# Mamba, MoE and attention on one core: softplus in halves, delta products between half down products, another order of ScalarE's copies and TensorE's turns, and a different start and end of the first stage

## The chip, the cores and the metric

One core of one Trainium2 chip runs the kernel. The metric is the device time in microseconds of one execution; lower is better. The kernel before was timed three times: median 3909.57, from 3905.14 to 3912.57. The engines are TensorE (PE, its weight loads PEld), VectorE (DVE), ScalarE (ACT), GpSimd (POOL) and SyncE (SP), whose instruction stream here issues all DMAs.

## The reference

Two layers are computed for 4096 tokens (batch 2, length 2048) of width 256. All is fp32.

- Mamba block: `xz = norm(x) @ W_in`, split in `x_br` and `z` of width 512; `xb = silu(conv4(x_br))`; `B, C = xb @ W_b, xb @ W_c` (16 states); `delta = softplus(xb @ W_delta + b_delta)`; for each of 16 states `h_t = exp(delta * A) * h_(t-1) + delta * B * xb`, `y = sum(h * C) + xb * D`; `out = (y * silu(z)) @ W_out + x`.
- Mixture of experts: a router (256 to 512, gelu, 512 to 4, softmax), the best two of four experts weigh `gelu(x @ We1) @ We2` (256 to 1024 to 256) per token; residual and norm around it.
- Attention with 16 heads of 16 per batch, keys with an added term from cross products of rotated values and keys, then an FFN (256 to 1024, relu, to 256), each with a norm.

## The kernel before, in words

The program has two blocks, one after the other. `mamba_moe_qkv` does all up to q, k and v; `attention_ffn` the rest. In each, every engine has its own stream, written out by hand and tied to the others by semaphores; each engine runs its stream in order. So a wait at one place holds up all that stands behind it on that engine.

**The chunk loop.** Tokens come in 8 chunks of 512 (`CH`). Features of width 512 are 4 blocks (`DB`) of 128 partitions. `iteration(i)` runs for i = -1 to 9 (3 to 5 in a hardware loop) and treats four chunks at once: i in the scan, f = i + 1 (its projection, conv, B/C and delta), m = i - 1 (out projection, norm 1, router, experts), q = i - 2 (norm 2, v, q, k, cross). It has 16 slots n, one for each state. In a slot DVE does for each of four blocks `b_times` (L1169: du times the broadcast B row, in PSUM) and `scan` (L1176), then `keep_state` (L1182); POOL multiplies by C (L1373) and adds to y (L1384); ACT has computed the decays (L876) one slot ahead; PE broadcasts row n + 2 at the slot's end (L577), for which it waits until DVE has done slot n's products. All other work is hung on slots, by `if n == ...` in each engine's `iteration`:

- **Slot 0:** DVE reads expert 3's down products 6 and 7 of chunk q (`down`, L1254) and computes `gated(m)` (L1188), all behind its scans; PE does these two down products.
- **Slots 1 and 2:** PE `project_out(m)` (L639), which waits for down product 7 to be read; `turn_x2`, `project_v` (L736, L727), `project_z` (L609). ACT `norm2`, `copy_v` (both copies of x2 and of v, L990, L993), `gates` (L890), `norm1` (L113).
- **Slot 3:** PE `project_qk` (turns of v, then q and k), `turn_x1` (L648), `turn_xn` (L586). ACT decays of slot 4 first, then `copy_qk` (v_tok L998, q and k L1005), `copy_x1` (L964), `copy_xn` (L896).
- **Slots 4 to 6:** `project_x(f)` (L597) in two pairs of blocks through PSUM banks 4 and 5, `copy_x` on ACT (L906, L907), `conv` on DVE (L1129, twelve instructions per chunk); cross products and router (L657, L664), logits, weighing. PE adds keys (L781), DVE takes them in slot 7 (`keys`, L1271).
- **Slots 6 to 15:** experts. `up(m, e, half)` (L694): 4 products in 3 side banks, each read by a gelu on ACT (L968); `down(m, e, pair)` (L717): two halves of 16 matmuls. Down products 0, 2, 4, 6 wait for the expert's last two gelus. DVE reads down product j one slot later. Down product 0 also waits for DVE's L1271.
- **Slots 11 to 15:** `project_bc` (L616), and `project_delta` 0 to 3 (L626) in slots 12 and 13, all through bank 5, around one down product in each slot. `copy_delta` on ACT (L928, L929) frees the bank; `softplus` in slot 14 does Exp on both halves (L935), then Ln on both (L939). ACT loads a table when it goes from one of Silu, Gelu, Exp and Ln to another. PE's slot 14 has the fourth expert's first up products and the bias products `base` (L684), which DVE adds in slot 15 (L1241). DVE splits B/C in slot 14 (L1137 to L1144) and computes delta and du at slot 15's end (`deltas`, L1154, L1160).

**The start.** SP loads eight Mamba tensors with x behind the fourth, under one semaphore `w_mamba`; PE, ACT and DVE wait for all of them. DVE's statistics of chunk 0 stand behind that wait. Iteration -1 holds only chunk 0's projection, conv and delta.

**The end.** Iterations 8 and 9 have no scans. In them the attention's first head is begun: `START` says how many steps `start_head` stand in a slot, each two score matmuls on PE (L561) and a maximum over them on DVE (L1110), 49 in all, through one pair of banks; step 36 is a turn (L553), behind which `load_neg` may run. `set_stacks` and `first_loads` (three heads, 13 DMAs each) prepare the operands in iteration 8, slots 3 and 5. The second block begins when the first has ended on all engines, stores included.

The lines that hold the order around the edit:

```python
if n in (12, 13) and inside(f):
    project_delta(f, 2 * (n - 12))
if n in (12, 13) and inside(m):
    down(m, 2, n - 12)
if n in (12, 13) and inside(f):
    project_delta(f, 2 * (n - 12) + 1)
```

## Time and profile before

| what | us |
|---|---|
| median of 3 runs | 3909.57 |
| the profiled execution | 3902.91 |
| its span | 3900.8 |
| busy: PE, DVE, ACT, POOL | 3424.4, 2953.6, 2202.5, 1521.5 |
| weight loads (beside PE) | 1588.6 |
| mean granted TensorE clock | 0.942 |
| first block | 0 to about 2083 |
| one iteration in the hardware loop | 228.66 |

Rows of a timeline read: start, duration, engine, line, operation, output<-inputs, shapes, count; in brackets the engine's idle time before it and who ended it. Neighbouring instructions of one kind are one row, so its duration spans all of them. Matmul ends are modelled and overlap their neighbours. "ps" is PSUM, "stacks", "vals" and "heads_v" are large buffers that hold delta, xb, y and others in the first block, and "hid", "soft", "q_f" are reused as well.

### The profile page before, as it was taken

To read this page: it belongs to the slowest core of one execution; us is meant where nothing else is said; L and a number is where in the kernel's file an instruction comes from. 1 tells how busy PE (TensorE), PEld (TensorE's weight loads), DVE (VectorE), ACT (ScalarE), POOL (GpSimd) and SP (SyncE) were. 2 spreads that over 40 slices of the span, in tenths; PEclk is the share of its full clock that TensorE was granted. 3 is DMA by queue.
4 is the path that set the end of the run, shared out by engine and by line. 5 is a ranking of instruction groups with operands and counts; after the bars stand their busy time and mean duration, and the time that the engine had idled before them with its cause. 6 is when DMAs were issued, how large, how long until landed. Compare 5 with 4: busy or idle time off the path is not lost. (4 is left out here: it accounts for less than half of the span.)

```text
span 3900.8 us, 50068 instructions
## 1 busy us (share of the span) xinstructions
PE 3424.4 (88%) x14561; PEld 1588.6 (41%) x14561; DVE 2953.6 (76%) x3565; ACT 2202.5 (56%) x3624; POOL 1521.5 (39%) x1294
## 2 busy tenths in 40 slices
PE   3238989898898979889988999999999999999898
PEld 1114545455454545546542333323323333333566
DVE  3898787887878788796337888888878888887343
ACT  3436455554646555463215777777777777776221
POOL 0988778787878887797100000000000000000110
PEclk8669999899999989999998999999999999999999
DMA  2111213122121311223301000000000000001010
GB/s 97 33 33 54 60 57 106 57 76 73 55 82 57 106 57 58 69 75 105 107 19 66 18 18 18 18 19 20 22 16 21 18 18 18 18 18 34 22 32 27
DMA packets 110809, 183.02 MB, mean 47 GB/s; under 512 B 14608, under 2 KB 84648, under 8 KB 101866
## 3 DMA queue, kind: packets, MB, share of 16 engines
q1 hardware_dynamic: 110569, 180.13, 14.7%
q8 instruction: 114, 1.87, 0.2%
q14 instruction: 126, 1.02, 0.1%
HBM read 153.99 MB, written 26.09 MB: 46 GB/s over the span
## 5 line engine op out<-in xcount | busy, mean ns | idle before, releaser
L1830 DVE TENSOR_REDUCE tile_max<-ps 128x1 f32<-128x1024 f32 x1028 | 1211.4, 1220 | 246.4 <-PE ps L1621 243.6
L1771 ACT ACTIVATE probs<-ps 128x512 f32<-128x512 f32 x2056 | 1116.1, 598 | 372.4 <-PE ps L1635 346.7
L1373 POOL TENSOR_TENSOR vals<-vals,c_sb 128x512 f32<-128x512 f32 x512 | 685.0, 1369 | 321.7 <-DVE state L1182 321.6
L1176 DVE TENSOR_TENSOR_SCAN vals<-stacks,state,ps 128x512 f32<-128x512 f32 x512 | 655.1, 1280 | 105.9 <-POOL heads_v L1384 36.1
L1635 PE MATMUL ps<-stacks 101*128 101x512 bf16 x2056 | 708.8, 383 | 3.0 <-ACTq L1778 1.7
L1384 POOL TENSOR_TENSOR heads_v<-heads_v,vals 128x512 f32<-128x512 f32 x512 | 638.4, 1278 | 8.7 <-issue 0.2
L1621 PE MATMUL ps<-stacks 99*128 99x512 bf16 x2056 | 615.3, 380 | 0.0
L1645 PE MATMUL ps<-probs,heads_v 128*32 128x512 f32 x4096 | 546.3, 605 | 3.5 <-issue 3.5
L231 POOL COPY heads_v<-vals 128x256 f32 (+1 forms) x32 | 12.6, 400 | 1364.0 <-PE ps L1645 1329.0
L694 PE MATMUL ps<-x1T,e_w 128*128 128x512 f32 x1024 | 489.8, 626 | 58.6 <-ACT hid L968 58.6
L717 PE MATMUL ps<-e_w,hid 128*128 128x256 f32 x2048 | 458.5, 383 | 37.3 <-issue 18.2
L1635 PEld LDWEIGHTS ps<-stacks 101*128 101x128 bf16 x2056 | 198.2, 96 | 639.3 <-ACT probs L1771 431.7
L717 PEld LDWEIGHTS ps<-e_w,hid 128*128 128x128 f32 x2048 | 389.9, 191 | 115.9 <-issue 61.7
L968 ACT ACTIVATE hid<-ps,cols 128x512 f32<-128x512 f32 x288 | 190.2, 686 | 398.7 <-PE ps L694 382.8
L876 ACT ACTIVATE stacks<-stacks,neg_a 128x512 f32<-128x512 f32 x512 | 334.4, 713 | 119.5 <-DVE vals L1176 118.1
L1169 DVE TENSOR_TENSOR ps<-stacks,ps 128x512 f32<-128x512 f32 x512 | 353.9, 691 | 16.2 <-PE ps L577 1.3
L694 PEld LDWEIGHTS ps<-x1T,e_w 128*128 128x128 f32 x1024 | 200.3, 200 | 305.3 <-issue 216.6
L1621 PEld LDWEIGHTS ps<-stacks 99*128 99x128 bf16 x2056 | 201.6, 98 | 180.0 <-issue 2.8
L577 PE MATMUL ps<-bc,sel 96*128 96x512 bf16 x128 | 50.7, 405 | 146.8 <-DVE ps L1169 128.4
L1645 PEld LDWEIGHTS ps<-probs,heads_v 128*32 128x32 f32 x4096 | 80.6, 108 | 197.5 <-ACT probs L1771 178.6
L1254 DVE SCALAR_TENSOR_TENSOR x_tok<-ps,cw,x_tok 128x256 f32<-128x256 f32 x128 | 55.4, 474 | 128.3 <-PE ps L717 128.2
L727 PE MATMUL ps<-x1T,wqkv 128*128 128x512 f32 x192 | 109.0, 723 | 38.0 <-ACT hid L998 25.1
(181 smaller groups left out, 2961.3 us busy)
## 6 DMA issues: line engine op xcount, KB each, us to landing
e_w<-in_e_w SPq DMA_DIRECT2D x64, 1024.0 KB, 7.1
c_sb<-scratch_c SPq DMA_DIRECT2D x128, 256.0 KB, 3.5
stacks<-scratch_q SPq DMA_DIRECT2D x210, 64.0 KB
stacks<-scratch_k SPq DMA_DIRECT2D x210, 64.0 KB
scratch_q<-parts SPq DMA_DIRECT2D x16, 384.0 KB, 4.2
scratch_k<-parts SPq DMA_DIRECT2D x16, 384.0 KB, 4.2
xr<-scratch_x SPq DMA_DIRECT2D x10, 512.0 KB, 4.2
xn_tok<-in_x SPq DMA_DIRECT2D x8, 512.0 KB, 4.8
```

What stands on the lines that cost most here:

```text
L694: last = mm(bank(key), e_w1[:, e % 2, k, i * P:(i + 1) * P], x1T[:, k, :], start=k == 0, stop=k == KD - 1)
L717: last = mm(ps[:, DOWN_BANK[at], i * D:(i + 1) * D], hid[:, k, (2 * pair + i) * P:(2 * pair + i + 1) * P], e_w2[:, e % 2, k, :], start=k = ...
L876: fn(decay[:, n % 2, m, :], delta[:, m, :], ACT.Exp, scale=neg_a[:, n * DB + m:n * DB + m + 1]).then_inc(s["decay_ready"], 1)
L1169: v.tensor_tensor(ps[:, 0, :], du[:, m, :], ps[:, 2 + n % 2, :], ALU.mult).then_inc(s["bx_ready"], 1)
L1176: v.tensor_tensor_scan(h[:, n % 2, m, :], decay[:, n % 2, m, :], ps[:, 0, :], state[:, n, m:m + 1], ALU.mult, ALU.add).then_inc(s["h_ready ...
L1373: last = nc.gpsimd.tensor_tensor(h[:, n % 2, m, :], h[:, n % 2, m, :], c_sb[:, n % C_RING, :], ALU.mult)
L1384: last = nc.gpsimd.tensor_tensor(y[:, m, :], y[:, m, :], h[:, n % 2, m, :], ALU.add)
L1621: last = mm(ps[:, slot(side) + i, :], qs[0:K_MAX, j, t * P:(t + 1) * P], ks[0:K_MAX, j, k * CH:(k + 1) * CH], start=True, stop=True)
L1635: mm(ps[:, S_BANK[i], :], ks[0:K_ALL, j, step * P:(step + 1) * P], qs[0:K_ALL, j, qc * CH:(qc + 1) * CH], start=True, stop=True).then_inc( ...
L1645: last = mm(ps[qc * VW:(qc + 1) * VW, AV_BANK, :], vh[:, j, step, :], probs[:, step % 2, qc, :], start=step == 0, stop=step == KT - 1)
L1771: fn(probs[:, step % 2, qc, :], ps[:, S_BANK[i], :], ACT.Exp)\
L1830: v.tensor_reduce(tile_max[:, t, half:half + 1], ps[:, slot(side):slot(side) + PAIR, :].rearrange("p a n -> p (a n)"), AX.X, ALU.max).then ...
```

## The change

- `deltas` between half products: in slots 12 and 13 PE does a delta product, half a down product, a delta product, the other half.
- Softplus in halves: Exp and Ln of blocks 0 and 1 stand behind `copy_delta(2)` in slot 13, those of blocks 2 and 3 in slot 14.
- Gelu waits: a down product's first half waits for the last three gelus one by one at the k-steps that read them.
- Slot 0: DVE does down 6 and `gated` between its second and third block. `project_out` starts when down 6 is read, and waits for down 7 before its second half.
- Slots 2 and 3: ACT copies x2 before slot 3's decays, v_tok before norm 1, then q, xn, half of slot 4's decays, k, x1, the other half. PE turns v, projects q, turns xn, projects k, turns x1, does the first cross product. `turn_xn` no longer waits for chunk m's x1 copy; `project_x` does.
- B/C product: waits for each block's Silu.
- Chunk 0: x is loaded first; small tensors, the x half of W_in and the rest have a semaphore each; the norm does not wait for weights. The x projection has four banks (`FIRST_X`), so have the deltas (`FIRST_DELTA`), without waits between; `norm0(1)` moves to slot 1 of iteration 0.
- The end: steps of `START` move from iteration 9 to 8, and the last five stand in slot 1 of iteration 9; `set_stacks` does head 0 in slot 0, `first_loads` loads it in slot 2, the others follow in slot 5; `load_neg` in slot 3 of iteration 9.

```diff
-START = {(NCH, 8): 6, (NCH, 9): 6, (NCH, 10): 6, (NCH, 11): 4, (NCH, 12): 2, (NCH, 13): 2, (NCH, 14): 4,
-         (NCH, 15): 4, (NCH + 1, 2): 3, (NCH + 1, 3): 4, (NCH + 1, 4): 2, (NCH + 1, 9): M_FIRST - 43}
+START = {(NCH, 6): 4, (NCH, 7): 6, (NCH, 8): 6, (NCH, 9): 6, (NCH, 10): 6, (NCH, 11): 4, (NCH, 12): 2, (NCH, 13): 2,
+         (NCH, 14): 4, (NCH, 15): 4, (NCH + 1, 1): M_FIRST - 44}
+FIRST_X = [4, 5, 6, 7]
+FIRST_DELTA = [0, 1, 6, 7]
+        def x_bank(c, e):
+            return FIRST_X[e] if first(c) else 4 + e % 2
+        def delta_bank(c, m):
+            return FIRST_DELTA[m] if first(c) else 5
...
             def first_loads():
-                sp.wait_ge(sh.sems["setup"], 2)
...
-                for u in range(3):
-                    load_stack(sp, sh, scr, u, u)
+                sp.wait_ge(sh.sems["setup"], 2)
+                load_stack(sp, sh, scr, 0, 0)
+            def more_loads():
+                sp.wait_ge(sh.sems["setup"], 2 * ROT)
+                for u in range(1, 3):
+                    load_stack(sp, sh, scr, u, u)
...
             load_x(0)
-            for t, name in mamba_loads[4:]:
-                sp.dma_start(t[:], a[name]).then_inc(s["w_mamba"], 16)
+            for t, name in small_loads:
+                sp.dma_start(t[:], a[name]).then_inc(s["w_small"], 16)
+            sp.dma_start(w_in[:, :, 0:DI], a["w_in"][:, :, 0:DI]).then_inc(s["w_x"], 16)
+            for t, src in mamba_loads:
+                sp.dma_start(t, src).then_inc(s["w_mamba"], 16)
...
             def turn_xn(c):
-                at_least(pe, s["x1T_ready"], c - 1)
             def project_x(c, blocks):
+                if first(c):
+                    pe.wait_ge(s["w_x"], 16)
+                at_least(pe, s["x1T_ready"], c - 1)
...
             def project_bc(c):
-                pe.wait_ge(s["xb_ready"], (c + 1) * DB)
                 for k in range(DB):
+                    pe.wait_ge(s["xb_ready"], c * DB + k + 1)
...
             def project_out(c):
-                at_least(pe, s["down_read"], c * 2 * NE)
+                at_least(pe, s["down_read"], c * 2 * NE - 1)
                 for i in (2, 3, 0, 1):
+                    if i == 0:
+                        at_least(pe, s["down_read"], c * 2 * NE)
...
-            def down(c, e, pair):
+            def down(c, e, pair, parts=(0, 1)):
-                wait_read(pe, c, ("up", e, HB - 2))
-                wait_read(pe, c, ("up", e, HB - 1))
-                for i in range(2):
+                for i in parts:
                     for k in range(HB):
+                        if pair == 0 and i == 0 and k >= HB - len(SIDE):
+                            wait_read(pe, c, ("up", e, k))
...
                     if n == 3:
                         if inside(q):
-                            project_qk(q)
+                            turn_v(q)
+                            project_q(q)
+                        if inside(f):
+                            turn_xn(f)
+                        if inside(q):
+                            project_k(q)
                         if inside(m):
                             turn_x1(m)
-                        if inside(f):
-                            turn_xn(f)
+                        if inside(q):
+                            cross(q, 0)
...
-                    if n in (12, 13) and inside(f):
-                        project_delta(f, 2 * (n - 12))
-                    if n in (12, 13) and inside(m):
-                        down(m, 2, n - 12)
-                    if n in (12, 13) and inside(f):
-                        project_delta(f, 2 * (n - 12) + 1)
+                    if n in (12, 13):
+                        for part in range(2):
+                            if inside(f):
+                                project_delta(f, 2 * (n - 12) + part)
+                            if inside(m):
+                                down(m, 2, n - 12, (part,))
...
-            def softplus(c):
-                act.wait_ge(s["abs_ready"], (c + 1) * DB)
...
+            def soft_exp(c, i):
+                half = slice(2 * i, 2 * i + 2)
+                act.wait_ge(s["abs_ready"], c * DB + 2 * i + 2)
+                fn(soft[:, half], soft[:, half], ACT.Exp, scale=-1.0).then_inc(s["soft_ready"], 1)
+            def soft_log(c, i):
+                half = slice(2 * i, 2 * i + 2)
+                act.wait_ge(s["soft_ready"], c * 4 + 2 * i + 1)
+                fn(soft[:, half], soft[:, half], ACT.Ln, bias=1.0).then_inc(s["soft_ready"], 1)
...
                 for n in range(NS):
+                    if n == 2 and inside(q):
+                        copy_x2(q)
-                        if n + 1 < NS:
+                        if n + 1 < NS and n != 3:
                             decays(i, n + 1)
...
                             gates(i)
+                        if inside(q):
+                            copy_v_tok(q)
                         if inside(m):
                             norm1(m)
                     if n == 3:
                         if inside(q):
-                            copy_qk(q)
+                            copy_qk(q, "q", 0)
+                            copy_qk(q, "q", 1)
+                        if inside(f):
+                            copy_xn(f)
+                        if inside(i):
+                            decays(i, 4, (0, 1))
+                        if inside(q):
+                            copy_qk(q, "k", 0)
+                            copy_qk(q, "k", 1)
                         if inside(m):
                             copy_x1(m)
-                        if inside(f):
-                            copy_xn(f)
+                        if inside(i):
+                            decays(i, 4, (2, 3))
...
+                    if n == 13 and inside(f):
+                        copy_delta(f, 2)
+                        soft_exp(f, 0)
+                        soft_log(f, 0)
+                        copy_delta(f, 3)
+                    if n == 1 and first(i):
+                        norm0(1)
                     if n == 14 and inside(f):
-                        softplus(f)
+                        soft_exp(f, 1)
+                        soft_log(f, 1)
...
+                    if n == 0 and inside(q):
+                        down(q, NE - 1, 0)
+                    if n == 0 and inside(m):
+                        gated(m)
...
-                    if n == 0 and inside(q):
-                        down(q, NE - 1, 0)
-                    if n == 0 and inside(m):
-                        gated(m)
...
-            dve.wait_ge(s["w_mamba"], W_MAMBA)
+            norm0_stats(0)
+            dve.wait_ge(s["w_small"], W_SMALL)
```

## Rows read from the trace of the kernel before

**Rows 1.** Stretches, busy us (instructions) of each engine, then granted clock, DMA share, GB/s.

```profile
core 0: us, PE busy (x) PEld busy (x) DVE busy (x) ACT busy (x) POOL busy (x), PEclk, DMA share, GB/s
1153.25:1267.57 114.32, 96.36 (x301) 53.33 (x299) 101.81 (x129) 67.81 (x103) 93.77 (x82) 0.93 0.16 51
1267.57:1381.91 114.34, 104.03 (x334) 62.94 (x335) 85.84 (x106) 59.15 (x82) 91.08 (x73) 0.96 0.29 93
```

**Rows 2.** Timeline of PE around down product 0 of iteration 5.

```profile
1257.80 7.03 PE L694 MATMUL ps<-x1T,e_w 128*128 128x512 f32 x16
1267.67 0.67 PE L717 MATMUL ps<-e_w,hid 128*128 128x256 f32 x2 [2.84 <-issue]
```

**Rows 3.** Timeline of DVE: keys in slot 7, down product 5, base products.

```profile
1266.31 1.26 DVE L1271 TENSOR_TENSOR k_f<-ps,k_f 128x512 f32<-128x512 f32 x2
...
1359.30 0.88 DVE L1254 SCALAR_TENSOR_TENSOR x_tok<-ps,cw,x_tok 128x256 f32<-128x256 f32 x2 [4.70 <-PE ps L717]
...
1379.58 0.69 DVE L1241 TENSOR_TENSOR x_tok<-ps,x_tok 128x512 f32<-128x512 f32 x1 [4.40 <-PE ps L684]
1381.22 0.69 DVE L1241 TENSOR_TENSOR x_tok<-ps,x_tok 128x512 f32<-128x512 f32 x1 [0.94 <-PE ps L684]
```

**Rows 4.** Timeline of PE: down 2, then slots 13 to 15.

```profile
1299.22 1.10 PE L717 MATMUL ps<-e_w,hid 128*128 128x256 f32 x4 [0.82 <-issue]
...
1348.65 3.70 PE L626 MATMUL ps<-vals,w_delta 128*128 128x512 f32 x8 [1.14 <-ACT soft L929]
...
1359.09 3.60 PE L626 MATMUL ps<-vals,w_delta 128*128 128x512 f32 x8
...
1373.69 3.78 PE L694 MATMUL ps<-x1T,e_w 128*128 128x512 f32 x4 [5.63 <-ACT hid L968]
...
1381.11 9.20 PE L694 MATMUL ps<-x1T,e_w 128*128 128x512 f32 x16
```

**Rows 5.** Timeline of ACT in slot 14 of iteration 5.

```profile
1363.31 0.68 ACT L929 ACTIVATE soft<-ps,cols 128x512 f32<-128x512 f32 x1
1363.88 2.55 ACT L876 ACTIVATE stacks<-stacks,neg_a 128x512 f32<-128x512 f32 x4
1366.33 1.99 ACT L935 ACTIVATE soft<-soft 128x1024 f32<-128x1024 f32 x2
1368.34 1.28 ACT L939 ACT_TABLE_LOAD   x1
1369.64 2.00 ACT L939 ACTIVATE soft<-soft 128x1024 f32<-128x1024 f32 x2
```

**Rows 6.** Line L1129, what DVE waited for, us and times: iteration 2, then 5.

```profile
  ACT vals L907: 9.1, 4
...
  ACT vals L907: 3.6, 4
```

**Rows 7.** Timeline of PE in slot 3 of iteration 5.

```profile
1209.90 7.75 PE L727 MATMUL ps<-x1T,wqkv 128*128 128x512 f32 x12 [4.18 <-ACT hid L998]
```

**Rows 8.** Timeline of all engines in the first 60 us.

```profile
13.73 1.40 DVE L100 BATCH_NORM_STATS2 ln_stats<-xn_tok 128x6 f32<-128x256 f32 x4
...
33.02 5.40 PE L597 MATMUL ps<-xnT,w_in 128*128 128x512 f32 x8 [4.34 <-DVE vals L1129]
...
43.02 2.19 ACT L913 ACTIVATE vals<-vals 128x512 f32<-128x512 f32 x4 [2.42 <-POOL vals L1423]
...
57.36 3.70 PE L626 MATMUL ps<-vals,w_delta 128*128 128x512 f32 x8 [1.36 <-ACT soft L929]
```

**Rows 9.** The page's DMA issues: KB each, median us from issue to landing.

```profile
xn_tok<-in_x SPq DMA_DIRECT2D x8, 512.0 KB, 4.8
```

**Rows 10.** Timelines of PE (three rows) and SP in iterations 8 and 9.

```profile
1905.22 0.60 PE L561 MATMUL ps<-stacks 99*128 99x512 bf16 x2
...
2020.23 1.97 PE L736 MATMUL ps<-ident,x_tok 128*128 128x128 f32 x8 [6.72 <-ACT x_tok L113]
...
2080.26 1.03 PE L561 MATMUL ps<-stacks 99*128 99x512 bf16 x2 [1.32 <-DVE tile_max L1110]
...
2070.19 0.95 SPq L461 DMA_DIRECT2D scratch_k<-parts  x2
```

More of the change, by code:

```diff
@@ L620, in project_delta @@
             def project_delta(c, m):
-                if m == 0:
+                if m == 0 and not first(c):
                     pe.wait_ge(s["bc_copied"], c + 1)
-                else:
+                elif not first(c):
                     pe.wait_ge(s["abs_ready"], c * DB + m)
                 for k in range(DB):
-                    last = mm(ps[:, 5, :], w_delta[:, k, m * P:(m + 1) * P], xb[:, k, :],
+                    last = mm(ps[:, delta_bank(c, m), :], w_delta[:, k, m * P:(m + 1) * P], xb[:, k, :],
                               start=k == 0, stop=k == DB - 1)
@@ L869, in _, with decays @@
             fn = nc.scalar.activation
-            def decays(c, n):
-                for m in range(DB):
+            def decays(c, n, blocks=range(DB)):
+                for m in blocks:
                     if n == 0 and m == 0:
@@ L999, in copy_qk @@
                             bank(("v_tok", i)), ACT.Copy), ("v_tok", i))
-                act.wait_ge(s["bc_steps"], 5 * (c + 3 if not isinstance(c, int) else min(c + 3, chunks)))
-                for j, (name, dst) in enumerate((("q", q_f), ("k", k_f))):
+            def copy_qk(c, name, m):
+                j, dst = (0, q_f) if name == "q" else (1, k_f)
+                if name == "q" and m == 0:
+                    act.wait_ge(s["bc_steps"], 5 * (c + 3 if not isinstance(c, int) else min(c + 3, chunks)))
+                if m == 0:
                     at_least(act, s["parts_steps"], 8 * c - 4 + 4 * j)
-                    for m in range(KD):
-                        wait_full(act, c, (name, m))
-                        read(fn(dst[:, m, :], bank((name, m)), ACT.Identity,
-                                bias=col("b" + name, m)), (name, m))
+                wait_full(act, c, (name, m))
+                read(fn(dst[:, m, :], bank((name, m)), ACT.Identity, bias=col("b" + name, m)), (name, m))
             def copy_cross(c):
```

115 lines of the change are left out of this document (60 added, 55 removed).

## The prediction

> **What bounds the kernel now.** The profiled execution took 3902.9 us, with a span of 3900.8. I read the page first, then DVE's idle times with their releasers, then TensorE's and ScalarE's timelines at those places, for the chunk loop, the start and the end of the first stage. The attention stage behind 2083 us has no edited line that runs in it.
>
> In the loop one iteration takes 228.66 us, and it falls into two legs that [rows 1] show with their busy times. I call "base" the moment at which DVE has added the second half of the bias product (1153.25, 1381.91), and "keys" the end of DVE's L1271 (1267.57). Leg A, base to keys, 114.3 us: DVE is busy for 101.8, PE for 96.4. PE's first down product of a chunk starts 0.10 us after L1271 ends, after 2.84 us of idleness: up to there DVE leads [rows 2, 3]. Leg B, keys to base, 114.3 us: PE is busy for 104.0, DVE only for 85.8, and DVE waits for PE, 4.70 us before it can read down product 5, then 4.40 and 0.94 before the base products [rows 3]. So time is won in leg A only by removing DVE's waits, in leg B only on PE's way to what DVE reads next.
>
> **Leg B.** (1) PE's order now is delta 0, down 4, delta 1; delta 2, down 5, delta 3. The new order puts delta 3 ahead of down 5's second half: DVE gets down 5 later by one delta product, 3.60 us [rows 4]. Against that, PE's wait of 1.14 before delta 2 goes, as half a down product (as many columns as a delta product) covers ScalarE's two copies, and the wait of 0.82 before down 2 goes, as its first five k-steps no longer wait for the last gelu [rows 4]. DVE reads down 5 now 91.7 us after keys (1359.30 - 1267.57), then 91.7 + 3.6 - 1.14 - 0.82 = 93.4.
> (2) From that read to DVE's arrival at base lie 15.9 us of its own work (1375.18 = 1379.58 - 4.40, less 1359.30), then two adds of 0.69 [rows 3]. That gives base at 93.4 + 15.9 + 1.5 = 110.8 if PE's base product is ready by 109.3.
> (3) Is it? Now the fourth up product waits 5.63 us for gelu, since ScalarE does both Exps (1.99 for two), an Ln load (1.28), two Lns and a Gelu load behind delta 3 [rows 4, 5]. In halves, Exp and Ln of blocks 0 and 1 take some 3.3 us and run while PE does delta 3. Behind it stand: copies 1.3, Exp load 1.28, decays 2.55, Exp 1.0, Ln load 1.28, Ln 1.0, Gelu load 1.28, one gelu 0.7 = 10.4. Delta 3 is over 95.1 us after keys now, then 95.1 - 3.6 (half a down product less ahead of it) - 2.0 (the two waits) = 89.5. So the fourth up product starts at about 100, with 1 of wait in place of 5.63, and PE does not fall to the lower clock there. Two products of some 1.9 later, at 104, base is ready, 5 us early. So the removed wait is mostly not paid out: DVE, delayed at down 5, is late next. Leg B gains 114.3 - 110.8 = 3.5 us. Bounds: -1.5 (all of (1)'s delay and none of its savings) and 5.3, what DVE now waits at base.
>
> ScalarE has two more table loads per chunk. The row has the load at 1.28 and the next activation right behind it (1368.34 + 1.28 = 1369.62, start 1369.64) [rows 5]. The Trainium skill (ScalarE: Activation LUTs, What ACT_TABLE_LOAD costs) gives about 2.66 us for a switch, a drain of 1.38 included; [rows 5] show no drain. By the skill's figure the start of the kernel, where this chain is bare, would be 2.8 us longer, and the loop the same.
>
> **Leg A.** (4) DVE waits four times per chunk for ScalarE's copies of the x projection: 9.1 us in iteration 2, 3.6 in iteration 5 [rows 6]; the same view gives 5.3, 3.5 and 5.7 for iterations 3, 4 and 6, together 27.2, and none in iterations 0 and 1. The new order (xn turned behind q, copied ahead of k and half of the decays, v's copies ahead of norm 1, which removes PE's wait of 4.18 [rows 7]) brings the x projection forward by 6 us. By my count its copies end 3 us before DVE gets there. I take 20 of the 27, as part may turn into waits for POOL. Bounds 10 and 27.
> (5) The price: PE does not need less time in leg A, so it waits longer for keys, 2.84 + 3 = some 5.8 us. The clock's rows: after 2.84 idle, no fall; after 4.18, twelve matmuls took 7.75 [rows 7] against three quarters of the 7.03 that sixteen take at full clock, 2.4 lost; after 5.63, four took 3.78 and sixteen 9.20, 4.2 lost, and by estimate 1.9 more in the base product between them [rows 2, 4]. The work behind keys is dense like that behind the 4.18; I take 2.6 in each of iterations 2 to 6, 13 in all, bounds 0 and 30. The Trainium skill (TensorE: Matmul & The Clock Gate, HAM oscillation) holds that such gaps, repeated, throttle the array every time. The rows at 4.18 and 5.63 agree, the one at 2.84 does not; by the rule alone the rival without a fall, below, would be out.
> (6) The gate in mid slot 0 only reorders DVE's work; it removes a wait of PE before the out projection. But PE's broadcast for slot 2 waits for DVE's last product of slot 0, so PE idles ahead of it instead; DVE needs the result only some 5 us later. 0. The earlier x2 copies on ScalarE delay the decays of slot 3, which have 10 us of slack. 0. The v, q, k and cross work only changes places.
>
> Loop: iteration 1 has only leg B's gain and a second gelu wait, 4; iterations 2 to 6 give 5 x 3.5 + 20 - 13 = 24.5; iteration 7 (no next chunk) 1; iteration 0, whose DVE waits only for POOL, 0. Sum 29.5.
>
> **The start.** The norm of chunk 0 starts at 13.73, behind all Mamba weights [rows 8]. With x issued first (at about 0.8) and landing after 4.8, the median of its loads [rows 9], it starts at 5.6: 8.1. Four banks for x: PE's wait of 4.34 [rows 8] and DVE's for those copies go, 5. The B/C product starts behind the first Silu instead of the fourth: three quarters of 2.19, 1.6. Deltas in four banks: three waits of 1.36 before a delta product [rows 8] and slack beside each, 5. Softplus behind the last delta: 0.4 longer. Sum 19.3; the clock, already high when the second half of x comes, adds a bit: 20. The chain from here to the scans is serial, so it counts in full. Bounds 15 and 24.
>
> **The end.** The first stage's last iteration begins for PE at 2013.5 (2020.23 less 6.72) [rows 10]. PE's last score pairs, 2.36 apart, run until 2082.6, though the k stores were issued at 2070.19 [rows 10]; they land after some 4 us, by the 4.8 of x. Now 15 such steps stand in this iteration, then 5, all at its head: PE's turn of x2 comes 5.5 later (5 x 2.36 less the idle 6.72 there), the later pairs no longer stand between (some 4 + 7), a lower clock costs 2, so keys and the k store come about 5 earlier and end the stage at 2070: 12.6. The ten steps moved to iteration 8, bound by PE, cost at most the 0.60 of such a pair [rows 10], some 0.44 as it overlaps its neighbours, and 1.5 where the first waits for the router's small work, 5.9; earlier gate and finer gelu waits there give back 3.3. Stack loads start earlier on SP, ahead of the v store, and none of these is late. Net 10; bounds 4 and 16.
>
> **Sum.** 29.5 + 20 + 10 = 59.5: 3902.9 - 59.5 = 3843.4 for a profiled run. The runs' median is 3909.6, 6.7 above the profiled one: 3850.1, and I say 3849.
>
> **The rivals.**
> - Deep clock fall (0.20): PE loses some 6 in each iteration behind keys, and half of (4) is not won: 17.5 + 10 - 30 leaves the loop near 0. Then 20 + 10 + 4 = 34: 3875. For it: 5.63 idle did cost 6.1. Against: that row had the small base products behind it, keys has not.
> - No fall and all waits gone (0.15): 59.5 + 13 + 7 = 79.5: 3830. For it: 2.84 of idle cost nothing.
> - The halves do nothing (0.05): ScalarE reaches delta 3's copy late, PE's wait of 5.63 stays. Then base comes 2 us after my time in five iterations, 10 lost: 3860. It would show as ScalarE busy with Ln at delta 3's end.
> - Slower (0.04): after the long wait for keys, TensorE stays at 1.2 GHz deep into leg B. It decides only from (59.5 + 13 + 8) / 5 = 16 us lost per iteration, 32 at the lower clock, where 12 is about the most that [rows 4] show (from 1373.69 into the 9.20). 3918 or more.
> - My case (0.56): 3849, its own range 3837 to 3865.
>
> About 0.2% (8 us) is what a measurement of this kernel can tell from no change. Faster 0.94, same 0.02, slower 0.04. Range: the deep fall with poor ends (3879) to no fall with good ends (3825).
>
> **What would show it.** Chunk 0's first scan some 20 us earlier. PE idle before the fourth up product down to 1 or 2, DVE's 4.40 at base gone, its wait for down 5 longer. DVE's waits for L907's copies near 0. PE's wait before down 0 at 5 to 6 us with a clock dip behind it. The first stage's end near 2025. An iteration of 224 instead of 228.7. I am wrong if DVE waits for ScalarE's decays in slots 3 or 4, or if iterations stay at 228.

## The result, and the profile after

The changed kernel took 3820.94 us (median of 4, 3819.2 to 3823.07), the kernel before 3911.07 beside it (3905.14 to 3913.17): a ratio of 0.977, 95% interval 0.9755 to 0.9789. The direction was right, the size was not: the time lies 28 us below the forecast and 4 below the range. The profiled executions are 83.7 us apart (3902.9 and 3819.2), where the sum said 59.5.

The windows of the changed kernel's iteration 5, from base to keys and from keys to base, in the columns of [rows 1]:

```profile
core 0: us, PE busy (x) PEld busy (x) DVE busy (x) ACT busy (x) POOL busy (x), PEclk, DMA share, GB/s
1101.69:1211.48 109.79, 87.45 (x288) 50.07 (x286) 100.73 (x128) 65.98 (x100) 91.77 (x82) 0.95 0.16 53
1211.48:1323.67 112.19, 107.75 (x348) 65.57 (x349) 85.89 (x107) 63.49 (x85) 91.06 (x73) 0.98 0.28 94
```

Leg A fell from 114.3 to 109.8, leg B from 114.3 to 112.2, and DVE's busy time hardly moved in either. So DVE's waits went, not its work.

Timeline of TensorE at keys, then in slots 13 to 15, which answers to [rows 2, 4]:

```profile
1202.64 2.74 PE L722 MATMUL ps<-x1T,e_w 128*128 128x512 f32 x6
1211.58 9.57 PE L746 MATMUL ps<-e_w,hid 128*128 128x256 f32 x32 [6.21 <-issue]
...
1299.51 3.60 PE L651 MATMUL ps<-vals,w_delta 128*128 128x512 f32 x8
1302.95 3.62 PE L746 MATMUL ps<-e_w,hid 128*128 128x256 f32 x16
...
1313.66 1.98 PE L722 MATMUL ps<-x1T,e_w 128*128 128x512 f32 x4 [1.72 <-ACT hid L1005]
1315.57 1.99 PE L712 MATMUL ps<-e_b,cwT 4*128 4x256 f32 x8
1317.49 7.13 PE L722 MATMUL ps<-x1T,e_w 128*128 128x512 f32 x16
```

The wait ahead of the fourth up product is 1.72 us instead of 5.63, and the base products behind it run at the full clock, 1.99 us instead of 3.78. In return the wait for keys is 6.21 instead of 2.84, and down product 0 behind it takes 9.57 instead of 7.14.

DVE in the same places, which answers to [rows 3]:

```profile
1210.22 1.26 DVE L1333 TENSOR_TENSOR k_f<-ps,k_f 128x512 f32<-128x512 f32 x2
...
1292.61 0.88 DVE L1316 SCALAR_TENSOR_TENSOR x_tok<-ps,cw,x_tok 128x256 f32<-128x256 f32 x2 [8.55 <-PE ps L746]
...
1306.60 0.88 DVE L1316 SCALAR_TENSOR_TENSOR x_tok<-ps,cw,x_tok 128x256 f32<-128x256 f32 x2 [4.62 <-PE ps L746]
...
1322.40 1.26 DVE L1303 TENSOR_TENSOR x_tok<-ps,x_tok 128x512 f32<-128x512 f32 x2
```

DVE no longer waits at base (4.40 and 0.94 before). The later half down products show at down product 4, for which DVE waits 8.55 instead of 5.11, and not at down product 5 (4.62 against 4.70). TensorE's base products end at 1317.56, and DVE adds them at 1322.40: 4.8 us of slack.

The convolution's line over the whole run, all iterations, before (L1129) and after (L1191); its waits, us and times:

```profile
  ACT vals L907: 46.0, 24
```

```profile
  ACT vals L944: 13.4, 2
```

In the loop nothing is left of them: the two that remain are those of the start. Of the 46.0, 27.2 were in iterations 2 to 6 and the rest in the start.

The start (DVE, then ScalarE's softplus) and the end (TensorE and SP), which answer to [rows 8, 5, 10]:

```profile
4.57 1.41 DVE L100 BATCH_NORM_STATS2 ln_stats<-xn_tok 128x6 f32<-128x256 f32 x4 [3.49 <-DMA xn_tok<-in_x]
```

```profile
45.22 0.68 ACT L966 ACTIVATE soft<-ps,cols 128x512 f32<-128x512 f32 x1
45.92 1.28 ACT L971 ACT_TABLE_LOAD   x1
47.21 1.06 ACT L971 ACTIVATE soft<-soft 128x1024 f32<-128x1024 f32 x1
```

```profile
1998.10 0.59 PE L1699 MATMUL ps<-stacks 101*128 101x512 bf16 x1 [12.39 <-ACTq L1842]
```

```profile
1993.63 0.95 SPq L474 DMA_DIRECT2D scratch_k<-parts  x2
1997.91 0.39 SPq L198 DMA_DIRECT2D vals<-scratch_v  x1
```

Chunk 0's norm starts at 4.57 instead of 13.73. The second block begins at 1998.10, 4.5 after the k store was issued; before, it began at 2083.03, some 13 after the store, as the last score pairs were still running.

Where the 83.4 us of the span went. The stretches end with each iteration's last `keep_state`, which stands behind its last scan:

| stretch | before | after | gained | forecast |
|---|---|---|---|---|
| start and iteration 0 | 252.5 | 229.7 | 22.8 | 20 |
| iteration 1 | 215.5 | 210.4 | 5.1 | 4 |
| iterations 2 to 6 | 1149.2 | 1109.5 | 39.7 | 24.5 |
| iteration 7 | 202.3 | 199.0 | 3.3 | 1 |
| last `keep_state` to the second block | 263.5 | 249.3 | 14.2 | 10 |
| second block | 1817.8 | 1819.3 | -1.5 | 0 |

### The profile page after: what moved, and what is told of

Same layout as the page of the kernel before. It is cut to its first block and busy times, and to the rows that moved or that the text cites. A ratio compares the mean times of both kernels' runs of the same rounds, so it can differ in the third digit from the quotient of the medians.

```text
span 3817.4 us, 50051 instructions
## 1 busy us (share of the span) xinstructions
PE 3385.6 (89%) x14561; PEld 1587.7 (42%) x14561; DVE 2945.8 (77%) x3571; ACT 2222.2 (58%) x3640; POOL 1508.8 (40%) x1294
## 5 line engine op out<-in xcount | busy, mean ns | idle before, releaser
L1437 POOL TENSOR_TENSOR vals<-vals,c_sb 128x512 f32<-128x512 f32 x512 | 673.0, 1346 | 275.9 <-DVE state L1244 275.8
L1699 PE MATMUL ps<-stacks 101*128 101x512 bf16 x2056 | 708.1, 382 | 13.6 <-ACTq L1842 12.4
L746 PE MATMUL ps<-e_w,hid 128*128 128x256 f32 x2048 | 472.2, 389 | 38.4 <-issue 33.4
L722 PE MATMUL ps<-x1T,e_w 128*128 128x512 f32 x1024 | 467.5, 601 | 35.4 <-ACT hid L1005 35.4
L746 PEld LDWEIGHTS ps<-e_w,hid 128*128 128x128 f32 x2048 | 399.8, 196 | 120.0 <-issue 62.2
L722 PEld LDWEIGHTS ps<-x1T,e_w 128*128 128x128 f32 x1024 | 192.2, 192 | 264.5 <-issue 196.6
L651 PE MATMUL ps<-vals,w_delta 128*128 128x512 f32 x256 | 117.9, 606 | 7.2 <-ACT soft L966 4.0
```

What stands on the lines that cost most here:

```text
L722: last = mm(bank(key), e_w1[:, e % 2, k, i * P:(i + 1) * P], x1T[:, k, :], start=k == 0, stop=k == KD - 1)
L746: last = mm(ps[:, DOWN_BANK[at], i * D:(i + 1) * D], hid[:, k, (2 * pair + i) * P:(2 * pair + i + 1) * P], e_w2[:, e % 2, k, :], start=k = ...
L1437: last = nc.gpsimd.tensor_tensor(h[:, n % 2, m, :], h[:, n % 2, m, :], c_sb[:, n % C_RING, :], ALU.mult)
L1699: mm(ps[:, S_BANK[i], :], ks[0:K_ALL, j, step * P:(step + 1) * P], qs[0:K_ALL, j, qc * CH:(qc + 1) * CH], start=True, stop=True).then_inc( ...
```

## The experiments

For all kernels I took the two legs of iterations 2 to 6 from DVE's timeline, and DVE's waits for ScalarE's copies in them. Here, and wherever a leg of the experiments is named, leg A ends with the last instruction of `keys`, 0.8 us behind the end of L1271: so leg A is 0.8 longer and leg B 0.8 shorter than in [rows 1]. Sums over the five iterations:

| kernel | median, us | against before | leg A | of it waits | leg B |
|---|---|---|---|---|---|
| before | 3911 to 3917 | | 579.4 | 27.2 | 569.7 |
| changed | 3820.9 | -90.1 | 552.4 | 0 | 557.2 |
| e1 order alone | 3885.7 | -26.9 | 551.2 | 0 | 576.2 |
| e2 softplus, deltas, gelu waits | 3875.7 | -37.0 | 583.8 | 32.9 | 547.4 |
| e3 start alone | 3892.0 | -20.7 | 589.7 | 39.9 | 568.0 |
| e4 end alone | 3899.8 | -12.9 | 579.5 | 28.0 | 569.7 |
| e5 order undone | 3856.3 | -55.5 | 599.0 | 47.7 | 544.4 |
| e6 delta order undone | 3825.5 | -86.3 | 552.4 | 0 | 557.7 |
| e7 gap filled | 3807.8 | -104.0 | 552.5 | 0 | 544.8 |
| e8 up products hoisted | 3801.2 | -110.6 | 555.3 | 2.6 | 536.9 |
| e9 early split | 3786.0 | -127.2 | 552.6 | 0 | 526.7 |
| e10 hoist and split | 3769.1 | -144.2 | 552.6 | 0 | 503.4 |
| e11 fill and split | 3776.4 | -136.9 | 552.3 | 0 | 519.1 |
| e12 gate alone | 3914.1 | +0.9 | 590.5 | 38.6 | 569.7 |
| e13 gelu waits alone | 3887.3 | -29.4 | 585.2 | 35.2 | 551.9 |
| e14 halves alone | 3909.9 | -6.8 | 583.9 | 32.3 | 565.4 |

Leg A less its waits is 550 to 553 in every row: nothing else in the change touches it.

The row of before is one execution, and a fast one: it took 3902.9 where the medians are 3911 to 3917. e3 and e12 leave both legs' code as it was, but for finer waits of the B/C product and for the order in slot 0, and their traces hold 39.9 and 38.6 us of waits for copies. So 27.2 is likely less than a typical execution of before has; only one was traced.

**e1, the order of slots 2 and 3 alone.** From before, ScalarE's side; TensorE's slot 3 as in the change's diff:

```diff
-                        if n + 1 < NS:
+                        if n + 1 < NS and n != 3:
...
+                            copy_qk(q, "q", 0)
+                            copy_qk(q, "q", 1)
+                            copy_xn(f)
+                            decays(i, 4, (0, 1))
```

> The kernel before with one part of the change: the new order of slots 2 and 3 (ScalarE's copies, TensorE's turns), nothing else. Theory 1, as corrected by the trace after the change: all 27.2 us that DVE waited for ScalarE's copies of the x projection in iterations 2 to 6 go, and TensorE pays 2.5 us for the lower clock behind a longer wait for keys in each of them (12.5): 3911 - 15 = 3896, and the trace has 0 us of those waits and a wait of 5 to 6 us before down product 0. Theory 2, the sum on record (20 won, 13 paid): 3904. Rival: the order's gain comes only with the shorter leg B of the other parts, because an iteration is set by leg B alone; then no difference, 3911 within 8.

3885.7 us, ratio 0.9932 (0.9909 to 0.9955). All waits went, 28.2 us of leg A; the wait for keys was 3.1 to 6.4 us long, and leg B lost 6.5 (down product 0 took 8.83 instead of 7.14 in iteration 4). It won more than both sums. Between the profiled executions (3902.9 and 3884.3) it is 18.7; the rest is the distance of before's median from its profiled execution, which probably holds shorter waits than the others. The rival of no difference is out.

**e2, softplus, delta order and gelu waits.** From before, `softplus` in halves, `down` in parts with the three finer waits, the alternation in slots 12 and 13:

```diff
+                        soft_exp(f, 0)
+                        soft_log(f, 0)
...
+                        if pair == 0 and i == 0 and k >= HB - len(SIDE):
+                            wait_read(pe, c, ("up", e, k))
```

> The kernel before with softplus in halves, the delta products between half down products and the finer gelu waits, nothing else. Theory 1: leg B (keys to base) gets 4.65 us shorter in iterations 2 to 6 (the 2.15 that the changed kernel shows, with the 2.5 of its clock fall added back, as here the wait for keys stays at 2.84 us and has no fall), iteration 1 about 5 and iteration 7 about 3: 3911 - 31 = 3880. Theory 2, the sum on record (3.5 each, 4 and 1): 3888. Rival: leg B's gain is taken back in leg A, where DVE then waits longer for ScalarE's copies of the x projection: those waits grow above 27 us, and the time is above 3895.

3875.7 us, ratio 0.9903 (0.9881 to 0.9926). Leg B is 108.8 to 109.0 us in four iterations, 4.6 less than before as theory 1 had it. The waits in leg A are 32.9 against 27.2, as the rival said, but the time is 19 us below its bound; and as e3 and e12 show 39.9 and 38.6 with an unchanged leg B, the 5.7 can't be put down to the shorter one. In iteration 5 leg B is 111.9. Timeline of TensorE at keys in iterations 3 and 5:

```profile
799.30 7.14 PE L718 MATMUL ps<-e_w,hid 128*128 128x256 f32 x32 [2.83 <-issue]
...
1249.40 10.13 PE L718 MATMUL ps<-e_w,hid 128*128 128x256 f32 x32 [2.84 <-issue]
```

The same two stretches as windows (PEclk is the third number from the end):

```profile
799.30:806.30 7.00, 7.00 (x33) 6.08 (x34) 6.62 (x9) 3.40 (x5) 1.79 (x2) 1.00 0.00 1
1249.40:1259.40 10.00, 10.00 (x33) 8.21 (x34) 8.67 (x11) 6.38 (x9) 4.80 (x4) 0.70 0.00 1
```

Two equal waits, and only behind the second was the clock at 1.2 GHz for part of the stretch (0.70 on average), which cost 3.0 us.

**e3, the start alone.** From before, the loads, semaphores and banks of chunk 0:

```diff
-                    if e < 2:
+                    if e < 2 or first(c):
...
+            load_x(0)
```

> The kernel before with chunk 0's shorter way alone (loads of x first, semaphores of their own, four banks, B/C product behind each Silu). Theory 1: the stretch up to the end of iteration 0 shrinks by what the changed kernel shows, 22.8 us, all of it in the start, so 3888. Theory 2, the sum on record: 20, 3891. Rival: part of the 22.8 came from the other parts in iteration 0 (softplus in halves), and the start alone gives 18 or less: 3893 or more.

3892.0 us, ratio 0.9949 (0.9931 to 0.9966), at theory 2's number. Up to the end of iteration 0 it won 21.6 (252.5 to 230.9) and 2.8 and 3.0 in iterations 1 and 2; then the steady iterations were 232.0 long instead of 228.8, with 7.7 to 9.2 us of waits for copies in each, so that the profiled executions are only 13.5 apart. That does not show a cost of the edit: of its code only the finer waits of the B/C product run there, leg B is 113.55 as before, and the medians are 20.7 apart, nearly the whole 21.6. Most likely the long iterations are the usual ones and the traced execution of before had short ones.

**e4, the end alone.**

```diff
+START = {(NCH, 6): 4, (NCH, 7): 6, ...
...
-                    if n == 5 and isinstance(i, int) and i == chunks:
+                    if n == 2 and isinstance(i, int) and i == chunks:
                         first_loads()
```

> The kernel before with the end part alone (steps of the first head moved from iteration 9 to 8 and to slot 1 of iteration 9, stacks and loads in two parts, negation's load in slot 3), the gelu waits as before. Theory 1: the first stage ends 14.2 us earlier in the changed kernel by this part, of which some 3 are the gate's and the gelu waits' in iteration 8, and the attention stage gives 1.5 back: 3911 - 10 = 3901. Theory 2: all 14 are this part's, 3898. Rival: the steps moved to iteration 8 are in TensorE's way there and cost as much as they win: 3907 or more.

3899.8 us, ratio 0.9965 (0.995 to 0.9979). Its last `keep_state` ends at 1820.1 and its second block begins at 2069.76, 249.7 later instead of 263.5: 13.9 us, so theory 2's share holds, and the median's 12.9 agrees. Keys come at 2057.0 instead of 2061.4; counted from that `keep_state`, which is 0.6 later than before, this is the 5 that was forecast.

**e5, the order undone in the changed kernel.** The reverse of e1's edit.

> The changed kernel with the new order of slots 2 and 3 taken back. Theory: leg A gets DVE's waits for ScalarE's copies back, 27 to 40 us in iterations 2 to 6 (27.2 in the kernel before, 32.9 with the softplus part alone, 39.7 with the start alone), leg B gets its clock falls back as won, up to 12.5. So 3821 + 33 - 12 = 3842, between 3835 and 3850, with leg B at 109 to 109.5 us where the granted clock does not fall. Rival: the parts only add up, so the order is worth the 27 us that it brought alone: 3848 or more. Second rival: the order is worth nothing beside the other parts, 3825 or less.

3856.3 us, above the theory's window: the order is worth 35.3 here, 26.9 alone. Its convolution line waits over the whole run:

```profile
  ACT vals L935: 61.0, 22
```

Less the 13.3 of the start that is 47.7 in the loop, above the 27 to 40 of the theory. Less the clock's 12.8 (557.2 to 544.4 in leg B) it is 34.9: this is the order's whole price. It is 20.5 more than in the trace of before, but only some 8 to 9 more than in those of e3 and e12, and by the medians the order is worth 8.4 more here than alone, where e1's own interval reaches 9 us either way. So the old order gives back some 8 of the 25 us that leg B wins, by this evidence, and not 20.

**e6, the delta order undone in the changed kernel.**

```diff
-                    if n in (12, 13):
-                        for part in range(2):
-                            if inside(f):
-                                project_delta(f, 2 * (n - 12) + part)
-                            if inside(m):
-                                down(m, 2, n - 12, (part,))
+                    if n in (12, 13) and inside(f):
+                        project_delta(f, 2 * (n - 12))
+                    if n in (12, 13) and inside(m):
+                        down(m, 2, n - 12)
+                    if n in (12, 13) and inside(f):
+                        project_delta(f, 2 * (n - 12) + 1)
```

> The changed kernel with delta, whole down product, delta in slots 12 and 13 again; softplus stays in halves. Theory: the alternation itself costs DVE 2.5 us at down product 5 (3.6 later, 1.14 won) and only buys slack in front of the base product. Undone, DVE reads down 5 some 2.3 us earlier after keys; TensorE's wait before the fourth up product of slot 14 grows from 1.7 to about 5 us, so its base product is ready within 1 us of DVE's arrival. 2 us less in each of iterations 2 to 6: 3821 - 10 = 3811. Rival: the alternation is what lets the base product be early; without it DVE waits at base again, with the clock fall behind the 5 us, and leg B is as long as before or longer: 3821 to 3833.

3825.5 us, 4.5 slower than changed, within the rival's range; my theory of 10 us less was wrong. TensorE and DVE in slots 14 and 15:

```profile
1320.24 3.38 PE L722 MATMUL ps<-x1T,e_w 128*128 128x512 f32 x4 [5.17 <-ACT hid L1005]
1323.55 1.99 PE L712 MATMUL ps<-e_b,cwT 4*128 4x256 f32 x8
```

```profile
1324.79 1.49 DVE L1303 TENSOR_TENSOR x_tok<-ps,x_tok 128x512 f32<-128x512 f32 x2 [2.59 <-PE ps L712]
```

DVE read down product 5 3.0 us earlier after keys (91.35 against 94.33) and then waited 2.6 for base. So the alternation trades one for the other: 1.7 us in each of iterations 1 and 7, and 0.5 over the five between.

**e7, the wait for keys filled.** Surplus matmuls, with the broadcast of row 8 moved behind them; nothing is left out.

```diff
+                    if n == 7 and inside(q) and inside(f):
+                        at_least(pe, s["bx_ready"], DB * (i * NS + 7))
+                        for _ in range(24):
+                            mm(ps[:, 2, :], sel[:, 8:9].to_broadcast([6 * NS, P]), bc3[:], start=True, stop=True)
+                        broadcast(i, 8)
```

> The changed kernel in which TensorE, between its last up product of slot 7 and down product 0, repeats the broadcast of row 8 twenty-four times into the same bank (surplus work, it only fills the wait for keys in iterations 1 to 6). Theory: the wait of 6.2 us falls to about 1, the clock stays at 2.4 GHz, down products 0 and its neighbours take 7.1 us instead of 9.6, and leg B gets 2.5 us shorter in iterations 3 to 6 and a little in 2: 3821 - 11 = 3810. Rival: the fall is not tied to this wait, or TensorE's gain is lost where DVE waits anyway: 3818 to 3824. Second rival: the surplus matmuls run into the time of keys and delay down product 0: 3824 or more.

3807.8 us, 13.2 less than changed, as the theory had it. TensorE at keys:

```profile
1204.59 0.38 PE L598 MATMUL ps<-bc,sel 96*128 96x512 bf16 x1
1204.81 7.07 PE L746 MATMUL ps<-e_w,hid 128*128 128x256 f32 x32
```

7.07 instead of 9.57: the wait's clock price is 2.5 us per iteration, 12.4 in leg B's sum (557.2 to 544.8). The Trainium skill (TensorE: Matmul & The Clock Gate, HAM oscillation) advises against idle gaps between groups of matmuls; this pair of runs agrees. The gaps of its example are longer than e2's 2.83 and 2.84 us, so the one of these without a fall does not speak against it, nor does the row at 2.84 that the prediction counted so.

**e8, up products hoisted.** Three of expert 1's up products go ahead of down product 0.

```diff
+                        if n == 7:
+                            up(m, 1, 0, 0, 3)
...
+                if e == 1 and half == 0:
+                    act.wait_ge(s["down_mm"], c * 2 * NE + 2)
```

> The changed kernel in which three up products of expert 1 are done in the wait for keys, ahead of down product 0 instead of behind down product 1 (ScalarE's first gelu of that expert then waits for down product 1). Theory: TensorE sets leg B, so 5.3 us of useful work moved into the 6.2 us of idleness, with the 2.5 of the clock, make it 7.8 us shorter: DVE's waits for down 4 and 5 (8.55 and 4.62) hold 13.2, enough to take it. Five iterations and some for iterations 1 and 7: 3821 - 42 = 3779. Rival: another engine comes up first in leg B (DVE's own work, ScalarE's decays or POOL), and half of it is lost: about 3800. Second rival: ScalarE's gelus wait for down product 1 and stop the up products: 3815 or more.

3801.2 us: 19.7 less than changed, half of the theory's 42. Iterations 2 and 6 have leg B at 104.8, the three in the hardware loop 108.0 to 109.7. TensorE there:

```profile
1197.54 7.46 PE L722 MATMUL ps<-x1T,e_w 128*128 128x512 f32 x17
1204.83 7.07 PE L746 MATMUL ps<-e_w,hid 128*128 128x256 f32 x32
...
1221.16 2.54 PE L722 MATMUL ps<-x1T,e_w 128*128 128x512 f32 x4 [2.13 <-ACT hid L1007]
1223.63 1.89 PE L821 MATMUL ps<-soft,bqs 112*16 112x512 f32 x2
```

In those three TensorE starts down product 0 some 2 us after keys (in iteration 5, L1271's counterpart ends at 1202.57 and the product starts at 1204.83), right behind its up products, where it waited for keys before; and it waits 2.1 for the first gelu. In iterations 2 and 6 it is not late. The first rival was right on the size, but the engine that came up is TensorE itself, in leg A; why only in the three was not traced.

**e9, the split of B and C early.** DVE splits in slot 13 into `bc_new`, and slot 14 keeps one copy.

```diff
+                    if n == 13 and inside(f):
+                        split_bc(f)
...
                     if n == 14 and inside(f):
-                        split_bc(f)
+                        keep_bc(f)
```

> The changed kernel in which DVE splits chunk f's B and C in slot 13, in the 8.55 us that it waits there for down product 4, into a buffer of their own; slot 14 keeps one copy of that buffer. Theory: what is late before the base product is now DVE itself (TensorE has the base product ready about 4.9 us before DVE adds it). The split takes 6.5 us in slot 14, the copy that stays about 0.5 to 1.3, so DVE comes 4.9 us earlier to base in iterations 1 to 6: 3821 - 25 = 3796, with DVE's idle time before the base products at 0 to 1 us. Rival: TensorE or ScalarE needs the time, base is not ready earlier than DVE takes it, or POOL holds the scans: 3810 or more.

3786.0 us, 34.9 less than changed and 10 better than the theory. DVE from the split to base:

```profile
1268.09 1.24 DVE L1205 COPY q_f<-q_f 32x512 bf16<-32x512 bf16 x1
1269.35 1.65 DVE L1206 TENSOR_TENSOR q_f<-q_f 32x512 bf16<-32x512 f32 x1
1272.13 0.88 DVE L1321 SCALAR_TENSOR_TENSOR x_tok<-ps,cw,x_tok 128x256 f32<-128x256 f32 x2 [1.13 <-PE ps L747]
...
1291.32 0.29 DVE L1212 COPY bc<-q_f 96x512 bf16<-96x512 bf16 x1
...
1296.32 1.49 DVE L1308 TENSOR_TENSOR x_tok<-ps,x_tok 128x512 f32<-128x512 f32 x2 [0.61 <-PE ps L713]
```

The wait of 8.55 shrank to 1.13, the copy costs 0.29, and DVE waits 0.6 at base. What was late before base was DVE, as the trace said. Leg B won 30.5 in five iterations, 6.1 each. 3.7 of them are not the split's own: down product 0 behind the wait for keys took 44.8 in the five instead of 48.5, as less of it ran at the lower clock.

**e10, hoist and split.** Both edits.

> Both: three up products of expert 1 ahead of down product 0, and the split of B and C in slot 13. The hoist alone gave 20 us, with TensorE then reaching keys 1.5 us late in iterations 3 to 5. Theory: with it TensorE bounds both legs, so the early split of DVE adds little: about 3795. Rival: what a shorter leg B of DVE saves, 4.9 us per iteration, comes on top: 3776.

3769.1 us, ratio 0.9638 (0.9619 to 0.9658), the fastest of all. It beat the rival's sum: leg B fell to 503.4, so TensorE did not bound both legs.

**e11, fill and split.** Both edits.

> Both: the wait for keys filled with surplus broadcasts, and the split of B and C in slot 13. Theory: the clock's 2.5 us and DVE's 4.9 us per iteration are on one chain (TensorE to down 5, then DVE to base), so they add up: 3808 - 25 = 3783. Rival: as DVE comes earlier to base, TensorE's own work of the next leg A starts no earlier, so it reaches keys late and the fill only delays it: 3795 or more.

3776.4 us: 44.6 less than changed, where e7 and e9 alone gave 13.2 and 34.9. They add up but for 3.5 us, as one chain would have it; the 3.7 of the clock that e9 had already won fits what is missing.

**e12, the gate alone.**

DVE's side:

```diff
+                    if n == 0 and inside(q):
+                        down(q, NE - 1, 0)
+                    if n == 0 and inside(m):
+                        gated(m)
                     if n == 2 and inside(m):
                         norm1_stats(m)
```

> The kernel before with the gate part alone (down product 6 and the gated product between DVE's second and third block of slot 0, the out projection in two halves). Theory, as on record: 0, as it only reorders DVE's work of slot 0, 3912 within 5. Rival: it takes TensorE's wait before the out projection away and lets DVE's products overlap less with POOL's, which is part of the 0.9 us that leg A is shorter beyond the waits: 3907 or less.

3914.1 us, ratio 1.0011 (0.9999 to 1.0023): 0, as forecast. Its profiled execution shows how the waits for copies grow, 5.4 us in iteration 3 and 10.9 in 4. TensorE's first x projection in the two:

```profile
766.53 3.70 PE L597 MATMUL ps<-xnT,w_in 128*128 128x512 f32 x8 [1.32 <-ACT xnT L898]
...
998.08 5.26 PE L597 MATMUL ps<-xnT,w_in 128*128 128x512 f32 x8 [1.32 <-ACT xnT L898]
```

The windows of these rows:

```profile
766.50:770.20 3.70, 3.67 (x9) 1.75 (x10) 1.15 (x2) 3.14 (x6) 3.70 (x4) 1.00 0.00 0
998.10:1003.40 5.30, 5.30 (x9) 2.40 (x10) 0.75 (x1) 3.23 (x7) 5.22 (x6) 0.70 0.00 0
```

In one the granted clock is 1.00, in the other 0.70: the copies come late because the product that feeds them falls into a stretch that is partly at 1.2 GHz. It is not alone: this row is 1.6 us longer in iteration 4, and four others between base and the second pair of the x projection lose 3.3 together, all with a lower mean clock than in iteration 3 (the largest is v's product, 6.71 against 5.62 at 0.54 against 0.65). It stands 13 us behind the 4.18 us wait of slot 3 [rows 7]; whether that wait starts the stretch was not tried.

**e13, the gelu waits alone.**

```diff
-                wait_read(pe, c, ("up", e, HB - 2))
-                wait_read(pe, c, ("up", e, HB - 1))
...
+                        if pair == 0 and i == 0 and k >= HB - len(SIDE):
+                            wait_read(pe, c, ("up", e, k))
```

> The kernel before with the finer gelu waits alone. Leg B in company of halves and alternation is 5.0 us shorter at full clock; this part's share is open. Theory: TensorE reaches delta 3 some 1.0 us earlier (down product 2 starts at 29.9 us after keys instead of 30.9 in the traces), and all behind it on TensorE and ScalarE, the base product too, moves by as much: 1.0 in iterations 2 to 6, somewhat more in 1 and 7: 3913 - 7 = 3906. As on record 0.82 each: 3908. Rival: gelus set the pace elsewhere and nothing is gained: 3910 to 3916.

3887.3 us, ratio 0.9929 (0.9906 to 0.9953); 14.1 less between the profiled executions. Leg B is 3.2 us shorter where 1.0 was expected (110.4 against 113.55). Timeline of TensorE in slot 14:

```profile
1135.08 3.48 PE L694 MATMUL ps<-x1T,e_w 128*128 128x512 f32 x4 [5.63 <-ACT hid L969]
1138.49 1.99 PE L684 MATMUL ps<-e_b,cwT 4*128 4x256 f32 x8
```

The wait is still 5.63, but the clock is back 3.4 us later, and base takes 1.99 instead of 3.78 (before, the row at 1148.75 of the same iteration). So 1.1 comes from TensorE being early, and the rest, above all those 1.8, from the clock.

**e14, the halves alone.**

```diff
-                        softplus(f)
+                        soft_exp(f, 1)
+                        soft_log(f, 1)
```

> The kernel before with softplus in halves alone, in the old order of slots 12 and 13 and with the old gelu waits. Theory, by the trace of the changed kernel with its delta order undone, where TensorE's wait before the fourth up product of slot 14 was 5.17 us against 5.63 before: the halves hardly shorten the wait, but the lower clock behind it is shorter and base takes 1.99 us instead of 3.78, so leg B is 2 to 3 us shorter: 3913 - 13 = 3900. Rival: the clock's stretch was shortened there by the earlier fall at keys, which is not here; then leg B is 0.5 to 1 us shorter and the time 3908 or more, and the alternation carries nearly all of the 5.0.

3909.9 us, ratio 0.9986 (0.9974 to 0.9997). TensorE's wait is 5.17 instead of 5.63, base still takes 3.77, leg B is 0.5 shorter: the rival was right on leg B and on the time. That the alternation then carries nearly all of the 5.0 was not, by e13.

## Why the prediction was right or wrong

The sum was made against the profiled execution. Of the 24 us that it fell short there, 15.2 lie in iterations 2 to 6 (7.0 in leg A; 8.0 in leg B, which won 12.5 where the sum had 17.5 less 13), 2.8 in the start, 4.2 in the end, 1.1 and 2.3 in iterations 1 and 7, and the second block gave 1.5 back.

- **Step (4), the waits for copies, was mis-sized.** I took 20 of 27.2, "as part may turn into waits for POOL". None did: leg A fell by 27.0 (579.4 to 552.4). I also took them from one trace, and as if the rest of the change left them alone. With leg B shorter they are 47.7 (e5), so the order, priced at 20 less 13, is worth 35 in the changed kernel; alone it was worth 27 by the medians, give or take 9 (e1).
- **Steps (1) to (3), leg B.** The handover came as told: base ready 4.8 us early against 5, TensorE's wait down to 1.72, DVE last. What brought it did not: without the alternation the wait is 5.17 (e6, e14), so it is not the halves that shorten it. At full clock the leg is 24.9 us shorter in five iterations (569.7 to 544.8 in e7), 5.0 each against 3.5. The term that failed is the 0.82 for the gelu waits, which are worth 3.2 (e13), 1.1 by TensorE's earlier start and most of the rest by the clock at base; the halves, to which (3) gave the main role, bring 0.5 alone (e14), and the alternation is what is left, some 1.0, if the three add up (e2 against these two); it was not run alone, and undone in the changed kernel it costs only 0.1 per iteration in leg B (e6). DVE read down product 5 91.9 us after keys (e2) where the steps give 92.6 by the same measure; its two adds took 1.26, not 1.5. Iteration 6 had a fall of 1.8 of its own before, which I left out.
- **Step (5), the clock at keys, was right:** wait 6.21 against 5.8, price 2.5 against 2.6, shown by e7. That kills both clock rivals. The deep fall never came, and the rival without a fall came nearest in time (3830) by a cause that did not happen.
- **Step (6), the gate at 0, was right** (e12).
- **The start:** 22.8 against 20. x landed in 3.8 us instead of 4.8, so the norm came 9.2 earlier, not 8.1; the B/C product gave 2.8, not 1.6 (first Silu to its copy: 8.63 before, 5.85 after); the x banks 5.4 and the deltas 5.5 were priced at 5 each. By an estimate from the Trainium skill's figure (ScalarE: Activation LUTs, What ACT_TABLE_LOAD costs) the start would have been 2.8 longer; the load at 45.92 takes 1.28 and the Exp behind it starts 0.01 later, so no drain shows here either.
- **The end:** 14.2 against 10, all of it this part's (e4). In e4's iteration 9 it won 8.5 between base and keys where I counted 5, and iteration 8 paid 3.5 instead of 5.9.
- **From profiled execution to median.** I added the 6.7 by which the median of before lay above its profiled run. For the changed kernel this is 1.7, which is 5.0 of the miss. The kernel before ranges over 19 us in 13 runs (3899.6 to 3918.8), the changed one over 4 in 4. In the traces of kernels with the old order the waits for copies come to 27 to 48 us, and e12 shows one cause; they may well make the spread between executions too, but that was not traced.

The halves' rival (3860), the slower one (3918) and the deep fall are out as times; that the halves do next to nothing was right for the halves alone. Of the signs named, DVE's longer wait for down 5 did not come. The range was too narrow below, because its low end rested on one rival instead of on several terms each a little too small: leg A in full, leg B, start and end near their upper bounds, and a median that lies closer to its profiled run.

## What to carry to other kernels

When two legs of a loop hand over to each other, price a wait with the other leg already shortened: the wait may grow and take part of that gain, and the edit that removes it is then worth more than its rows say (here 35 us, where alone it brought 27, give or take 9). After a change, look for the engine that idles just before the point where another arrives last: DVE's 8.55 us before down product 4 could take 6.5 us of its own later work, and that alone (e9) gave 35 us. If a loop's waits hang on the granted clock, one profiled execution is a draw, and its distance from the median does not carry over to the changed kernel.

## What the runs showed of the hardware

The clock's fall does not follow from the length of the wait before it: two waits of 2.83 and 2.84 us in one run, with the same matmuls behind them, cost 0 and 3.0 us (e2). Nor does its length: behind 5.63 us of idleness the first twelve matmuls took 7.6 us (3.78 + 3.78) in the kernel before and 5.5 (3.48 + 1.99) with only the gelu waits changed (e13). In the first the granted clock was 0.50 over both rows and 0.73 over the next 7.9 us, in the second 0.56 over the first row and 1.00 from there on. What decides between them was not found; in e13 the row starts 1.1 us earlier after keys. So two kernels that differ by a small shift can differ by 2 us per iteration through the clock.
